# Earlier bias and row blocks between the first weight pieces, tile 3's turned rows between two products, and one weight quarter a step later

## What is computed

```
x = x + conv_block(layernorm_over_channels(x))     # gates, taps, group statistics, a DFT magnitude map
t = tokens(x)                                      # 2048 tokens of 256 channels
t = t + moe(layernorm(t))
moe: S = sigmoid(t @ Wg); G, I = top_k(S, 2)       # 8 experts
     h = gelu(t @ W1[e] + b1[e])                   # 256 -> 1024
     y = h @ W2[e] + b2[e]                         # 1024 -> 256
     out = sum over the two chosen experts of G * y
```

## Time and profile before

| | |
|---|---|
| median of the runs | 347.26 us (345.86 to 347.35) |
| the profiled execution | 349.64 us, of it 347.8 us span from first to last instruction |
| TensorE | 301.3 us busy (87% of the span) |
| VectorE | 251.8 us (72%) |
| ScalarE | 182.2 us (52%) |
| GpSimd | 155.1 us (45%) |
| granted TensorE clock, mean | 0.957 of full speed |

### The profile page before, as it was taken

The page is one execution under the profiler, slowest core; times in us unless marked ns, Lnnn a source line. Parts: engine busy times, 40 slices in busy tenths (PEclk is TensorE's granted clock), DMA queues, the critical chain, the costliest instruction groups (busy, mean ns, idle before and its releaser), DMA issues.

```text
span 347.8 us, 8621 instructions
## 1 busy us (share of the span) xinstructions
PE 301.3 (87%) x3022; PEld 225.6 (65%) x3022; DVE 251.8 (72%) x597; ACT 182.2 (52%) x506; POOL 155.1 (45%) x161
## 2 busy tenths in 40 slices
PE   0989989999920687999999989999999999999970
PEld 0767833557710366788888868888888888877740
DVE  3786789578899869988887798797855655655530
ACT  3344649444653427558576567667544353554410
POOL 7012770337531360454456354644554635444341
PEclk9989999999975699999999999999999999999996
DMA  7400000002286854367888678789454334233310
GB/s 235 145 1 2 1 0 1 2 0 82 69 288 205 160 164 173 97 148 227 190 206 212 158 168 225 214 183 237 90 90 82 66 73 80 49 69 62 57 17 2
DMA packets 36185, 39.41 MB, mean 113 GB/s; under 512 B 8400, under 2 KB 32816, under 8 KB 36144
## 3 DMA queue, kind: packets, MB, share of 16 engines
q1 hardware_dynamic: 29168, 29.56, 29.5%
q0 software_dynamic: 6976, 9.31, 15.9%
HBM read 29.74 MB, written 9.11 MB: 112 GB/s over the span
## 4 chain that ended last, share of the span: by engine, by line
PE 62%; DVE 16%; DMA 11%; issue 4%; ACT 2%; another core or an unknown queue 1%; SPq 1%; POOL 1%; POOLq 0%; ACTq 0%
PE ps L886 14%; PE ps L871 7%; PE ps L875 7%; PE ps L873 7%; PE ps L887 7%; DMA out<-fb,idx 6%; PE ps L731 5%; PE ps L712 3%; DMA wt<-w 2%; DMA xt<-x_tok 2%; PE ps L740 2%; PE ps L744 2%; PE ps L747 2%; PE ps L825 2%; PE ps L779 1%
## 5 line engine op out<-in xcount | busy, mean ns | idle before, releaser
L659 ACT ACTIVATE fb<-ps,b1t 128x128 f32<-128x128 f32 (+7 forms) x312 | 82.1, 381 | 71.6 <-issue 51.4
L871 PE MATMUL ps<-fb,wt 128*128 128x128 f16 (+7 forms) x624 | 114.4, 214 | 5.3 <-DVE fb L1296 5.3
L886 PE MATMUL ps<-wt,fb 128*128 x312 | 117.0, 379 | 0.0
L875 PE MATMUL ps<-fb,wt 128*128 128x128 f16 (+7 forms) x624 | 114.4, 214 | 0.3 <-issue 0.3
L873 PE MATMUL ps<-fb,wt 128*128 128x128 f16 (+7 forms) x624 | 114.3, 214 | 0.0
L523 POOL DMA_INDIRECT out<-fb,idx x39 | 65.3, 1674 | 101.7 <-DMA out<-fb,idx 69.8
L887 PE MATMUL ps<-wt,fb 128*128 x312 | 85.0, 272 | 0.0
L871 PEld LDWEIGHTS ps<-fb,wt 128*128 x624 | 60.9, 98 | 36.0 <-issue 6.2
L873 PEld LDWEIGHTS ps<-fb,wt 128*128 x624 | 60.4, 98 | 3.3
L875 PEld LDWEIGHTS ps<-fb,wt 128*128 x624 | 60.4, 98 | 0.5 <-issue 0.5
L513 POOL DMA_INDIRECT fb<-xn_rows,idx x39 | 43.6, 1117 | 25.0 <-DVE idx L1274 12.8
(11 more groups left out here) (204 smaller groups left out, 388.1 us busy)
## 6 DMA issues: line engine op xcount, KB each, us to landing
wt<-w SPq DMA_DIRECT2D x32, 512.0 KB
b2t<-b SPq DMA_DIRECT2D x39, 128.0 KB
xt<-x_tok SPq DMA_DIRECT2D x4, 512.0 KB, 7.8
out<-xt SPq DMA_DIRECT2D x8, 256.0 KB, 2.1
xn_rows<-wt SPq DMA_DIRECT2D x8, 256.0 KB, 3.3
b1t<-params SPq DMA_DIRECT2D x39, 4.0 KB
fb<-xn_rows,idx POOLq DMA_INDIRECT x39
out<-fb,idx POOLq DMA_INDIRECT x39, 4.0
```

The lines of the kernel that those rows point to most:

```text
L659: a = nc.scalar.activation(hid[:, s, f * P:f * P + ROWS[n]], h_ps(s)[:, f * P:f * P + ROWS[n]], ACT.Gelu_apprx_tanh, bias=b1t[:, n % NBIAS ...
L871: pe.matmul(dst, hi, xT[:, s, c * P:c * P + rows], start=(c == 0 and f % 4 == 0), stop=False, skip_group_check=True)
L875: m = pe.matmul(dst, lo, xT[:, s, c * P:c * P + rows], start=False, stop=(c == DC - 1), skip_group_check=True)
L886: pe.matmul(y_ps(s), hhi[:, s, f * P:(f + 1) * P], w, start=(f == 0), stop=False)
```

## The change

Three places change.

1. `quarters_at(1)` is empty now and `quarters_at(2)` is 4 and 5. All other rounds stay. Since SyncE, ScalarE and VectorE all use this function, three things move: the split of quarter 4 on ScalarE, its remainder on VectorE, and on SyncE the load of quarter 8.
2. At the start of the experts' part SyncE issues the loads of quarters 0 and 1, then the last block of normalized rows to DRAM, then tile 0's bias, then the loads of quarters 2 and 3, then the biases of tiles 1 to 3.
3. VectorE runs `gate_pay(2)`, `rows_T(3)`, `gate_pay(3)` in round 1, where it ran both products there and `rows_T(3)` in round 2.

```diff
-            upto = lambda n: min(QUARTERS_FIRST + 4 * n // 3, NQ)
+            upto = lambda n: min(QUARTERS_FIRST + 4 * n // 3, NQ) if n != 1 else QUARTERS_FIRST
             return range(upto(n - 1), upto(n)) if n > 0 else range(0)
...
-            for h in range(NSTG):
+            for h in range(DC):
                 load(h)
             rows_out(B - 1)
-            for i in range(NBIAS):
+            biases(0)
+            for h in range(DC, NSTG):
+                load(h)
+            for i in range(1, NBIAS):
                 biases(i)
...
-            def gate_pay():
-
-                for n in (2, 3):
-                    ins = v.tensor_tensor(out=pay[:, :, n, :], in0=pay[:, :, 0, :],
-                                          in1=over_tiles(flat(place16[:, n]), 2 * NBLK), op=ALU.mult)
-                ins.then_inc(hot_done, 1)
+            def gate_pay(n):
+
+                return v.tensor_tensor(out=pay[:, :, n, :], in0=pay[:, :, 0, :],
+                                       in1=over_tiles(flat(place16[:, n]), 2 * NBLK), op=ALU.mult)
...
                 if n == 1:
-                    gate_pay()
-                if 2 <= n < TILES - 1:
+                    gate_pay(2)
+                    rows_T(3)
+                    gate_pay(3).then_inc(hot_done, 1)
+                if 3 <= n < TILES - 1:
                     rows_T(n + 1)
```

## The result

The changed kernel takes 351.72 us, the median of 4 runs (350.49 to 352.51). The kernel before, run beside it on the same chip, takes 346.59 us (345.86 to 347.35, 4 runs). The ratio is 1.0145, with a 95% interval of 1.0099 to 1.019: slower by about 5 us. The forecast was 351.9 us.

What follows compares the result with a forecast made beforehand. The experts' part was taken to go at TensorE's pace. Starting step 8 4.6 us late, with nothing given back, added 4.6 to 347.3 for 351.9 us; likeliest range 351.0 to 353.0, with rivals 348.7 to 353.8.

Steps and rivals of the forecast that it cites:

- Part 2, the load of quarter 8: SyncE issues this load behind the wait for y_done 2, 4.98 us later; this decides the forecast loss of 4.6 us.
- The landing: Time from quarter 8's late issue until it lands: 5.6 us taken, the middle of 4.82 and 6.38 us.
- The stall at step 6: TensorE waits about 4.6 us there for work behind quarter 8's late load; step 6 starts 3.6 us late.
- The stall at step 8: New TensorE stall of 1 us, as quarters 10 and 11 come 5.5 us late; step 8 starts 4.6 us late.
- the clock: Rival: TensorE's granted clock falls after the new stall, costing 0 to 1.5 us, up to 353.4 us; chance 0.05.
- Part 1, step 3's 1.1 us: Quarter 4's remainder (1.14 us on VectorE) leaves the way to step 3, which starts at 138.66 instead of 139.80.
- the rival of quarter 8 hidden: Faster if the landing takes under 2.8 us; with the wait gone, 2.7 us gained, 344.6 us; chance 0.06.
- Part 3, the bias: Moving tile 0's bias ahead of quarters 2 and 3 gains 0; bounds 0 and about 1.8 us gained.
- The hole: Gap of 3.44 us before the first gelu, taken as ScalarE lacking its instructions; expected to stay about 3.4 us.
- My reading of the wait instruction: ScalarE's wait (L655) shows at 128.54 and takes 0.02 us, read as coming late rather than waiting.
- The bias rival: The gap before the first gelu is the wait for its bias: loss 2.8 us, 350.1 us; chance 0.13.
- The late stall: Rival: TensorE's 1.50 us stall ending at 201.94 goes, as its load may have landed: +3.1 us, 350.4; chance 0.11.

Runs made afterwards that it cites:

- e6: Kernel before, with SyncE's loads alone by the new table, so quarter 8 loads behind the wait for y_done 2: 351.63 us, ratio 1.0134.
- e1: Changed kernel, with SyncE's loads by the old table again, splits and remainders as changed: 347.34 us, ratio 0.9982.
- e2: Kernel before, with the quarters' table alone changed (quarter 4 split and quarter 8 loaded in round 2): 351.94 us, ratio 1.0134.
- e5: Changed kernel, with 16 matmuls on constants, output unused, on TensorE ahead of step 6: 350.84 us, ratio 1.0094.
- e7: Changed kernel, with each SyncE round's loads ahead of its biases, so ahead of that round's wait for y_done: 347.23 us, ratio 0.9976.
- e0: Kernel before, profiled once more with no edit: 345.04 us, one run.
- e4: Kernel before, with tile 3's turned rows alone moved between the two products of gates and payload: 346.88 us, ratio 0.9963.
- e9: Changed kernel, with SyncE's loads by the old table and ahead of the biases in each round: 346.52 us, ratio 0.9969.
- e3: Kernel before, with the order of SyncE's requests at the start alone changed (rows and tile 0's bias between quarters 1 and 2): 346.91 us, ratio 0.9999.
- e8: Kernel before, with loads ahead of the bias in each of SyncE's rounds: 346.69 us, ratio 0.9972.
- e10: Kernel before, with tile 3's turned rows between the two products and SyncE's loads ahead of the bias: 347.51 us, ratio 1.0009.

## Why the prediction was right, point by point

**Part 2, the load of quarter 8: right, and shown to be the whole of it.** e6 makes the loss with the request alone, e1 takes it away. Within the profile after, y_done 3 comes 154.26 - 144.17 = 10.09 us behind y_done 2; the prediction's working had 157.4 - 147.3 = 10.1. The landing was 5.34 us (151.09 - 145.75) against the 5.6 taken, and 4.91, 4.61, 4.75 and 4.65 us in e2, e5, e6 and e7. So the company behind cost 0.5 us at most here against the 4.82 us of a lone quarter. The Trainium skill (DMA: Bandwidth & Descriptors, "Queues, rings and completion order") has descriptors on each DMA engine consumed in ring order. The five landings agree with it, but the next pair doesn't bear it out: quarter 10, with quarter 11 behind it, took 6.38 us before, 5.58 us after (161.12 - 155.54) and 5.6 to 7.1 us in e0, e1, e2, e5 and e6. Why it takes longer than quarter 8 isn't shown.

**The stall at step 6: right.** 3.98, 4.04 and 2.88 us against about 4.6.

**The stall at step 8: it didn't come, and the clock took its place.** These are the two terms of the sum that failed. I gave it 1.0 us beyond step 6's lateness, and gave the clock 0.05 and at most 1.5 us. The clock cost 1.8 (e2, e6) to 2.9 us (after). TensorE at half clock ate the slack ahead of step 8, so that gelu 6 waited 1.44 us for TensorE instead of the reverse. With the clock held up in e5, 0.46 us are lost at step 8. The two errors cancel in part: 3.98 + 2.94 = 6.92 us from step 5 to 7 in the profile after and 5.85 in e2, against 4.6 + 1.0 = 5.6 forecast for both steps together.

**The number: luck has a share in it.** 351.9 forecast and 351.72 measured are 0.2 us apart. But the loss forecast was 4.6 us on a median of 347.3, and the loss measured is 5.1 us on one of 346.59. The totals agree better than the terms inside them. A small slip of the working had no effect: for a landing of 4.82 us its sum gives +3.8 us, not +3.9.

**Part 1, step 3's 1.1 us: right at step 3; whether it is ever kept is open.** With the table's line (e2, e1) step 3 comes 1.0 to 1.1 us earlier than in e0; with the rows moved alone (e4) not at all. It is quarter 4's remainder that was in the way, as forecast. And where the load is late it isn't passed on, as forecast (e2 against e6). The working kept the gain wherever the stall at step 6 would be absent (the rival of quarter 8 hidden). Where nothing stalls at step 6 (e1, e7, e9), the ratios of 0.9982, 0.9976 and 0.9969 fit a gain of 1 us (0.997) and none alike. One profile of each shows steps 7 to 16 in 50.9 to 51.5 us, against 49.5 to 51.1 us in the profiles without the new table, which is too wide a spread to decide it.

**Part 3, the bias: right in value, and the cause wasn't tested.** e3 shows 0.9999. The hole was in one profile of before and in none of the other thirteen (e0 is the same program), so the row that I explained by late instructions was an accident. What made it isn't shown. My reading of the wait instruction failed too: its row takes 17 ns in the profiles before, after and e0 alike, behind the hole and behind a true wait of 1.69 us, so its length doesn't say whether ScalarE waited. The bias rival falls: the hole is gone without the bias moved. That the hole was missing in the profile after, which I had named as a sign against me, proved nothing, because a single profile can lack it.

**The late stall: gone in the profile after, but not shown to be that rival.** The stall of 1.50 us at 201.94 isn't in e0 either, which reaches step 16 from step 7 in 49.68 us, like the profile after (49.49), where the profile of before took 51.14. Whether it comes is a matter of the execution.

**The other side, quarter 8 hidden: excluded.** No landing of a late-requested quarter 8 took less than 4.6 us.

**No version beats the kernel before clearly.** The best, e4, e9 and e8, read 0.996 to 0.997. The intervals of e8 and e9 hold 1; e4's ends at 0.9997, and e10 with the same edit reads 1.0009.

## What to carry to other kernels

A table that several engines share moves more than the step one looks at. Before moving a piece of work, list every queue in which it has an entry, the DMA queue first, and see which wait it is moved past. A request that slips behind a wait costs its lateness less the user's slack: in e6 it came 5.3 us later after tile 0's turn than in e0 (24.85 against 19.58), and the stall was 2.88 us. Here such a stall of TensorE cost about half its length again or more in clock (1.8 us for 2.88 and for 4.04, 2.9 us for 3.98). Look a hole or stall of one profile up in a second profile of the same program before building on it.

## What the runs showed of the hardware

- In e6 a stall of 2.88 us on TensorE, in the middle of full work, was followed by the 1.2 GHz level (0.50) from about 158.2 to 161.7 us. The granted clock still read 1.00 during the stall itself and for over a microsecond behind it (TensorE by windows):

```profile
155.00:156.00 1.00, 0.00 (x0) 1.00 0.07 4
...
157.00:158.00 1.00, 1.00 (x15) 1.00 0.41 112
158.00:159.00 1.00, 1.00 (x10) 0.62 0.76 214
159.00:160.00 1.00, 1.00 (x8) 0.50 1.00 311
```

Idle time and its price stand at different places of the timeline. The price was half of the time that TensorE worked at this level: 1.7 us of 3.4 in e6 (1.8 measured). In the profile after the level fell 1 us before the stall had ended and held longer, so that 5.8 us were worked at it and 2.9 lost.
- Adds with indices to DRAM, one tile of up to 128 rows of 1 KB each, stand in e7's chain with 4.2 to 7.5 us each between 164 and 237 us, while weights were loading.
- 27 runs of the kernel before on one chip lay between 344.33 and 349.05 us. With a spread of 1.4% one pair of profiles can't carry a difference of 1%.
